# Kernel with an S4D convolution and three feed-forward layers: another order in SBUF for the convolution's input

## What is computed

```python
def layernorm(x): ...                       # over the channels
def ffn_fft(x, w):                          # a product in frequency = x @ M, M built from w
    return real(ifft(fft(x) @ w)) + bias
def s4d(u, log_tau, log_dt, mix, D):        # u: (B, C, T)
    E = exp(-(tau * dt)[:, None] * t[None, :]); K = mix @ E
    y = irfft(rfft(u, 2 * T) * rfft(K, 2 * T))[..., :T]     # causal convolution over time
    return y + D[None, :, None] * u

x = x + 0.5 * ffn_fft(layernorm(x))
v = layernorm(x)
h = layernorm1(v) * norm1_w + norm1_b       # h is the convolution's input u
v = v + s4d(h)
g = gelu(layernorm2(v) @ fc1.T + fc1_b) @ fc2.T + fc2_b
x = x + (v + g)
x = x + 0.5 * ffn_fft(layernorm(x))
```

## Time and profile before

| | |
|---|---|
| median of 3 runs | 2309.11 us (2308.8 to 2309.48) |
| span of the profiled execution | 2308.2 us; what lies around it isn't given apart: the median is 0.9 us over the span |
| mean granted clock of TensorE | 0.952 |
| stage 1, preparation | 0 to about 150 us (a few tiles of stage 2 lie in it) |
| stage 2, feed-forward and the convolution's input | about 150 to 533.1 us |
| stage 3, convolution | 533.1 to 715.4 us |
| stage 4, with the transfers ahead of it | 715.4 us to the end |
| busy over the span | PE 89%, PEld 45%, DVE 58%, ACT 33%, POOL 26% |

### The profile page before, as it was taken

How to read it: one execution, slowest core, us unless ns; L and a number is a source line. 1 busy time by engine, 2 the same in 40 slices (tenths; PEclk the granted TensorE clock), 3 DMA queues, 4 the chain that set the end, 5 groups by cost and what they waited for, 6 DMA issues and landing times.

```text
span 2308.2 us, 28297 instructions
## 1 busy us (share of the span) xinstructions
PE 2051.8 (89%) x10596; PEld 1028.8 (45%) x10596; DVE 1333.5 (58%) x2099; ACT 765.5 (33%) x939; POOL 593.6 (26%) x416
## 2 busy tenths in 40 slices
PE   7925667637986999999999999999999999999998
PEld 5412323215754444444444444444444444444443
DVE  4837999997887653726536264362644626446242
ACT  2335767765554221312213032130311303123020
POOL 0226777765433120201102011020110202102011
PEclk8968898978988999999999999999999999999999
DMA  6154322214979001011010110101101011010000
GB/s 220 3 156 162 125 91 73 91 50 116 283 229 305 23 19 37 19 55 37 20 37 19 56 37 19 37 19 55 37 20 37 19 54 35 23 37 19 19 19 19
DMA packets 112301, 157.54 MB, mean 68 GB/s; under 512 B 23731, under 2 KB 58035, under 8 KB 111412
## 3 DMA queue, kind: packets, MB, share of 16 engines
q1 hardware_dynamic: 112181, 155.77, 21.3%
HBM read 100.69 MB, written 63.41 MB: 71 GB/s over the span
## 4 chain that ended last, share of the span: by engine, by line
PE 74%; DVE 8%; issue 5%; POOL 5%; DMA 3%; SPq 3%; ACT 2%; DVEq 0%; POOLq 0%; ACTq 0%
PE psum L1535 29%; PE psum L1556 29%; PE psum L1407 8%; PE psum L1399 2%; PE psum L1461 2%; DVE arena L1056 2%; POOL taps L556 2%; SPq L351 2%; POOL taps L553 1%; ACT arena L704 1%; POOL va L525 1%; DMA arena<-in_x 1%; PE psum L1370 1%; PE psum L1452 1%; DMA w_scratch<-arena 1%
## 5 line engine op out<-in xcount | busy, mean ns | idle before, releaser
L1535 PE MATMUL psum<-arena 128*128 128x512 f16 x3072 | 677.4, 380 | 1.9 <-DVE arena L1266 1.5
L1556 PE MATMUL psum<-arena 128*128 128x512 f16 x3072 | 665.7, 379 | 0.0
L799 ACT ACTIVATE arena<-psum,b1p,sc 128x512 f32<-128x512 f32 x256 | 199.1, 778 | 1038.4 <-PE psum L1535 1038.4
L1556 PEld LDWEIGHTS psum<-arena 128*128 128x128 f16 x3072 | 300.6, 98 | 362.2
L1535 PEld LDWEIGHTS psum<-arena 128*128 128x128 f16 x3072 | 300.6, 98 | 353.5 <-issue 7.0
L525 POOL TENSOR_TENSOR va<-va,mhalf 128x4 f32<-128x4 f32 x80 | 106.8, 1338 | 1343.2 <-DVE va L918 1291.8
L1333 DVE SCALAR_TENSOR_TENSOR arena<-psum,sc,arena 128x512 f32<-128x512 f32 x64 | 48.1, 751 | 579.4 <-PE psum L1556 579.4
L1407 PE MATMUL psum<-m_parts,taps 128*128 128x512 f16 x768 | 210.4, 432 | 104.7 <-DVE taps L1048 93.4
L1310 DVE SCALAR_TENSOR_TENSOR arena<-arena,sc 128x512 f16<-128x512 f32 x256 | 243.9, 953 | 9.1
L1056 DVE TENSOR_TENSOR arena<-taps,arena 128x512 f16<-128x512 f32 (+1 forms) x64 | 166.6, 2606 | 63.5 <-ACT arena L704 63.3
L1307 DVE TENSOR_SCALAR arena<-arena,sc 128x512 f16<-128x512 f32 x256 | 140.2, 548 | 107.4 <-ACT arena L799 107.1
(11 more groups left out here) (157 smaller groups left out, 1865.4 us busy)
## 6 DMA issues: line engine op xcount, KB each, us to landing
arena<-in_x SPq DMA_DIRECT2D x16, 1024.0 KB, 9.8
x_scratch<-arena SPq DMA_DIRECT2D x16, 1024.0 KB, 4.5
taps<-taps_copies SPq DMA_DIRECT2D x64, 256.0 KB, 4.1
y_scratch<-arena SPq DMA_DIRECT2D x32, 512.0 KB, 6.1
arena<-y_scratch SPq DMA_DIRECT2D x15, 1024.0 KB, 7.1
arena<-x_scratch SPq DMA_DIRECT2D x15, 1024.0 KB, 5.5
out<-arena SPq DMA_DIRECT2D x15, 1024.0 KB, 5.1
taps<-taps_copies SPq DMA_DIRECT2D x64, 128.0 KB, 4.6
```

The costliest lines, as they stand in the source:

```text
L799: act.activation(h32[:, hc % 4, :], bank(hc % 2), ACT.Gelu, scale=scale(C_W1), bias=b1p[:, hc:hc + 1])\
L1535: last = pe.matmul(bank(hc % 2), w1_sb[:, a, k, hc * P:(hc + 1) * P], gt[:, b, k, :], start=(n == 0), stop=(n == 3 * KC - 1))
L1556: last = pe.matmul(bank(4 + j % 2), hid[:, a, hc, j * P:(j + 1) * P], w2_sb[:, b, hc, :], start=(n == 0), stop=(n == 3 * HC - 1))
```

## The change

The order of `u_all` becomes block, tile, half, channel. A tile writes four runs of 128 neighbouring f16 elements for each half; the 64 tiles of one channel then lie 2 x 128 elements = 512 bytes apart. The matmuls of `states` read 8 channels by 64 tiles and those of `inside` 64 tiles of one channel, both with that step. The order of the columns in PSUM stays (channel outer, tile inner), so nothing else changes: the same instructions in the same order with the same waits on every engine.

```diff
-        u_all = area(REG, 4 * REG).bitcast(F16).rearrange("p (b s c t) -> p b s c t", b=BLOCKS, s=2, c=BLK)
-        u_flat = area(REG, 4 * REG).bitcast(F16)
+        u_all = area(REG, 4 * REG).bitcast(F16).rearrange("p (b t s c) -> p b s c t", b=BLOCKS, s=2, c=BLK)
 
             def u_part(o, part, channel, n):
 
                 blk, place = divmod(o, per_block)
-                at = ((blk * 2 + part) * BLK + place * OC + channel) * TILES
-                return u_flat[:, at:at + n]
+                at = place * OC + channel
+                return u_all[:, blk, part, at:at + n, :]
 
             def states(o, i):
...
-                    last = pe.matmul(bank(i), to_state[:, a, :], u_part(o, b, 0, OC * TILES),
+                    last = pe.matmul(bank(i), to_state[:, a, :], u_part(o, b, 0, OC),
                                      start=(n == 0), stop=(n == 2))
...
                         pe.matmul(bank(4 + i)[:, c * TILES:(c + 1) * TILES], taps[:, i, :, a, c],
-                                  u_part(o, b, c, TILES), start=(c == 0 and n == 0), stop=False,
+                                  u_part(o, b, c, 1), start=(c == 0 and n == 0), stop=False,
                                   skip_group_check=True)
```

## The result

The kernel after the change takes 2418.78 us (median of 4 runs, 2418.19 to 2419.3), the one before 2309.29 us in the same comparison: ratio 1.0472, 95% interval [1.0459, 1.0485], 4.7% slower. Forecast were 2448 us. The span of the profiled execution is 2416.3 us, the mean granted clock of TensorE 0.889 against 0.952.

A forecast was written before the change was run, and what follows sets the result against it. It took DVE to bound stage 2 and PE stage 3. From 2309 us, -80 us for cheaper writes and +219 us for stepped reads gave 2448 us, slower by 6%; range for 8 in 10: 2240 to 2500 us.

The forecast's parts named there:

- Writes: Stage 2: packed writes save each tile about 1.85 us on DVE and 1.9 us on ACT.
- sum of turns: Stage 2: DVE and POOL alternate on operations with two SBUF inputs, 17.1 us a group; 17.8 us was taken.
- Part 1: Gain from packed writes ahead of stage 3: -80 us, between -55 and -100; ten groups 66, drain 10, first groups 4.
- x: Stage 3: TensorE's price per moving column 512 bytes apart, taken as 1.9 ns; chance 0.52 of 1.5 ns or more.
- low end: Stage 3: a stepped column costs 0.42 ns, or 0.48 ns as in PE's stepped weight load (61 ns for 128).
- `between`: Stage 3: these matmuls stay at 0.43 us a block; a clock fall to 1.2 GHz would double them, +27 us.
- Stage 3 before: In the kernel before the change, all 64 blocks of stage 3 take 182.3 us.
- part 2: Loss from stepped reads in stage 3: 401 us against 182.3 us, +219 us.
- Two packed columns' price: Rival in stage 3: a stepped column costs 0.84 ns, stage +24 us, total 2253 us, faster; chance 0.20.
- crossing at x = 1.19 ns: Stage 3 at 262 us, 4.1 us a block, uses up the writes' 80 us; below this price the kernel is faster.
- No loss at all: Rival in stage 3: a stepped column costs 0.42 to 0.48 ns, stage +0 to 6 us, total 2229 to 2235; chance 0.15.
- Writes that don't get faster: Rival in stage 2: the ring's operand causes L704's 2.6 us, write gain nil, each case 80 us later; chance almost nothing.

The follow-up runs named there:

- pool_quarter: The changed kernel with POOL's two steps per tile cut to 128 of 512 channels (wrong numbers): 2394.0 us.
- taps_packed: run2 with the 128 weights of each `inside` matmul read in one run instead of 32 bytes apart (wrong weights): 2210.4 us.
- run4: The changed kernel with groups of 4 neighbouring channels per tile: writes in runs of 8 bytes, TensorE reads with a step of 8 bytes: 2245.1 us.
- run2: The changed kernel with pairs of channels per tile: writes of 4 bytes, reads with a step of 4 bytes: 2221.79 us, ratio 0.9625 to the kernel before.

## Why the prediction was right, point by point

- **Bound of each stage.** Right: DVE in stage 2 and PE in stage 3, before and after (16.25 of 16.50 us; 395.67 of 395.70 us).
- **Writes.** 0.63 and 0.69 us measured for 0.68 to 0.76 us forecast. Ten groups at 16.6 us instead of 17.8: 78 us for 66. The sum of turns (17.1 us) was near, but partly by luck: pool_quarter takes about 8 x 0.81 = 6.5 us out of that sum and only 1.9 us out of the group, so the sum is not what sets the group; DVE's own work is. The 0.7 us put on top of it wasn't needed. The drain gave 15 us for 10, the first groups nothing for 4: the load of x still takes 22.5 us to land. Part 1: -93.4 us for -80, inside -55 to -100.
- **Reads.** x = 1.9 ns was taken from ACT's write with the same step; 1.67 in `states` and 1.80 in `inside` were measured, inside 1.63 to 2.05. That a wide step costs the reader some four packed columns held. That ACT's write gave nearly the right figure was in part luck: no run shows that the two accesses share a cause, and where the step is short they differ (at runs and steps of 8 bytes ACT writes at its full pace, 627 ns, while TensorE pays double, 0.89 ns a column). The low end (61 ns for 128 weights) was, as taps_packed shows, itself the price of a step.
- **`between`.** 0.43 us was taken for it; the clock at the 1.2 GHz level made it 0.85 us, the 27 us that the working set beside the sum. This error and the one in x nearly cancel, which is luck: 6.18 us a block for 6.27.
- **Stage 3 before.** This step failed. I read 715.4 us, where the chain passes from PE to SP, as the end of stage 3. Four blocks (96 of L1461's 1536 matmuls) are still to come there; PE ends at 725.1 us. Stage 3 had 192 us, not 182, so part 2 should have been 401 - 192 = +209 us and the forecast 2438 us. It measured +203.7.
- **Stage 4.** Unchanged, as forecast: 1563.2 us for 1563.3.
- **Sum.** 2448 us for 2418.8: 13 us from part 1, 10 us from the end of stage 3, 5 us from the price of a block with the clock in it, 2 us from the gap before stage 4; the medians differ by 1.4 us more than the spans, which takes that much off again.
- **Rivals.** Two packed columns' price, and the crossing at x = 1.19 ns: not reached with 512 bytes, but run4, at 0.89 ns in `states`, is nearly that rival and took 2245.1 us where 2253 was worked out for it; a block there is 1.36 + 1.55 + 0.43 = 3.34 us for 3.18, and the larger gain of the writes outweighs it. No loss at all: run2, 2221.8 us, for 2229 to 2235. Writes that don't get faster: 627 and 688 ns, with the same ring as operand, rule it out.

## What to carry to other kernels

When an order in SBUF is changed for the engine that writes, price the engine that reads by its own step, and look for an order in between: a few neighbours together may give the writer nearly all and cost the reader little. Here a pair of f16 elements did it, with four the reader paid double already, and both extremes lost to the pair. And read the end of a stage from its last instruction on the engine that bounds it, not from where the chain leaves that engine.

## What the runs showed of the hardware

- TensorE's moving f16 operand: 0.42, 0.44, 0.89, 1.75, 1.79 and 1.67 ns a column at steps of 2, 4, 8, 16, 32 and 512 bytes. At 512 bytes the price is the same at granted clocks of 1.00 and 0.50 (2.7 to 2.8 us for 24 x 64 columns at either).
- A weight load with a step of 32 bytes sets a pace of 61 ns, at clock 1.00 and 0.50; with the weights packed a load and its matmul of 64 columns take 30 ns at clock 1.00.
- ACT and DVE writing 512 f16 elements: 2.6 us one by one 128 bytes apart, 0.70 and 0.76 us in pairs, 0.63 and 0.69 us in runs of four and more. The odd price is that of a single f16 element, half of a 4-byte piece.
- A small DVE operation beside a POOL step lasts as long as that step: four elements take 1.24 us beside one of 1.27 us, 0.43 us beside one of 0.46 us.
- TensorE, busy all the time with stepped columns, was granted 0.50 (1.2 GHz) over stage 3 with both reads stepped, 0.71 with `states` alone, and 0.94 with `inside` alone or nothing stepped. The cause is open.
